# A second wait before the first exponential of every key tile, in a one-core attention kernel

## What is computed

```python
qkv = (x @ Wqkv_w + Wqkv_b).reshape(Bb, Ll, 3, Hh, dd)
scores = einsum('bhid,bhjd->bhij', q, k) * scale
attn = softmax(scores + causal_mask, axis=-1)
y_softmax = einsum('bhij,bhjd->bhid', attn, v)
def step(state, inp):
    q_t, k_t, v_t = inp
    state = retention * state + Gamma * (v_t[..., :, None] * k_t[..., None, :])
    return state, einsum('bhij,bhj->bhi', W_static + state, q_t)
alpha = sigmoid(gelu(x @ gate_w1 + gate_b1) @ gate_w2 + gate_b2)
y = alpha * y_softmax + (1.0 - alpha) * y_stp
x = x + (y @ out_w + out_b)
x = x + fp8_linear(layernorm(x), weight, bias)
```

## Time and profile before

| what | value |
|---|---|
| median of 3 runs | 1900.53 us |
| lowest and highest run | 1897.35, 1902.42 us |
| the profiled execution, its own time | 1900.53 us |
| its span, first to last instruction | 1898.8 us |
| granted TensorE clock, mean | 0.932 |
| PE, DVE, ACT, POOL busy | 89%, 82%, 71%, 64% of the span |
| middle stage, 178.9 to 1735.1 us | 1556.2 us |
| groups 2 and 3 of the middle stage | 379.2 and 382.5 us |

### The profile page before, as it was taken

One profiled execution on the slowest core, in us unless ns is written; L12 is line 12 of the kernel. 1 busy time (PEld: TensorE's weight loads), 2 busy tenths in 40 slices (PEclk: granted clock), 3 DMA queues, 4 the chain that ended last, 5 costly groups with the idle time before them and its releaser, 6 DMA issues. The chain is left out here.

```text
span 1898.8 us, 37291 instructions
## 1 busy us (share of the span) xinstructions
PE 1688.7 (89%) x13680; PEld 603.6 (32%) x13680; DVE 1551.2 (82%) x1709; ACT 1352.6 (71%) x2819; POOL 1223.0 (64%) x1146
## 2 busy tenths in 40 slices
PE   5996699999999999999999999999999999986633
PEld 3542122223333332233333322333323233323522
DVE  4457998998888899988888998989889999802967
ACT  2551288888886888888868887888678888894311
POOL 2102497768777777687777776877777788832535
PEclk9996599999998999999989999999989999997865
DMA  4674342241221421412214213122243121104402
GB/s 137 228 242 136 81 109 80 62 99 55 70 74 56 104 81 61 103 53 69 72 60 103 82 59 96 59 70 64 67 103 91 40 90 49 52 9 137 138 11 77
DMA packets 115176, 162.88 MB, mean 86 GB/s; under 512 B 29808, under 2 KB 57648, under 8 KB 114992
## 3 DMA queue, kind: packets, MB, share of 16 engines
q1 hardware_dynamic: 112608, 158.74, 28.7%
q10 hardware_dynamic: 2384, 1.77, 0.3%
HBM read 122.00 MB, written 38.01 MB: 84 GB/s over the span
## 5 line engine op out<-in xcount | busy, mean ns | idle before, releaser
L1399 DVE TENSOR_REDUCE pmax<-PS 128x2 f32<-128x1024 f32 (+2 forms) x1120 | 1213.6, 1130 | 147.0 <-PE PS L1203 117.1
L1351 ACT ACTIVATE probs<-PS 128x512 f32<-128x512 f32 (+3 forms) x2304 | 1124.6, 572 | 263.6 <-PE PS L1239 188.7
L1239 PE MATMUL PS<-Q_st,K_st 50*128 50x512 f16 (+3 forms) x1408 | 394.2, 366 | 15.8 <-DVE y_sb L1424 4.9
L1203 PE MATMUL PS<-K_st,Q_st 48*128 48x512 f16 (+3 forms) x1408 | 342.5, 362 | 13.4 <-DVE pmax L1399 11.3
L1260 PE MATMUL PS<-probs,V_g 128*17 128x512 f32 (+3 forms) x2816 | 346.1, 564 | 9.1 <-ACT o_t L1372 4.4
L1111 POOL TENSOR_TENSOR v_exp<-v_exp,k_rows 128x512 f32<-128x512 f32 x256 | 321.3, 1284 | 31.1 <-DMA v_exp<-qkv_t 30.4
L1153 POOL TENSOR_TENSOR state<-odd,q_rows 128x514 f32<-128x514 f32 x256 | 281.7, 1132 | 6.1
L1239 PE MATMUL PS<-Q_st,K_first 50*128 50x512 f16 (+3 forms) x896 | 270.5, 381 | 14.4 <-DVE shift L1414 6.9
L1203 PE MATMUL PS<-K_first,Q_st 48*128 48x512 f16 (+1 forms) x832 | 217.9, 406 | 25.3 <-DVE pmax L1399 23.7
L1260 PE MATMUL PS<-probs,V_first 128*17 128x512 f32 (+3 forms) x1792 | 232.4, 591 | 0.0
L1142 POOL COPY carry<-odd 128x4 f32<-128x4 f32 x64 | 12.0, 187 | 329.3 <-DVE odd L1434 329.3
(11 more groups left out here) (167 smaller groups left out, 1500.2 us busy)
## 6 DMA issues: line engine op xcount, KB each, us to landing
v_exp<-qkv_t SPq DMA_DIRECT2D x256, 256.0 KB
qkv_t<-proj SPq DMA_DIRECT2D x24, 512.0 KB, 3.8
qk_parts<-parts SPq DMA_DIRECT2D x16, 512.0 KB, 5.3
Q_st<-qk_parts SPq DMA_DIRECT2D x192, 32.0 KB, 3.8
v_rows<-vaug SPq DMA_DIRECT2D x8, 544.0 KB, 6.1
xin<-x SPq DMA_DIRECT2D x8, 512.0 KB, 6.2
k_rows<-qkv_t SPq DMA_DIRECT2D x16, 256.0 KB, 3.9
q_rows<-qkv_t SPq DMA_DIRECT2D x16, 256.0 KB, 6.2
```

The costliest lines, as they stand in the source:

```text
L1203: mm = pe.matmul(PS[:, bank, 0:width], Q_st[rows, c, pair, j * P:(j + 1) * P], keys[rows, pair, blk * CH:blk * CH + width], start=True, st ...
L1239: mm = pe.matmul(PS[:, bank, 0:CH - r * P], keys[rows, pair, kt * P:(kt + 1) * P], Q_st[rows, c, pair, r * P:CH], start=True, stop=(kt < T ...
L1351: act.activation(probs[:, tile % P_SLOTS, h, 0:CH - r * P], PS[:, step[5], 0:CH - r * P], ACT.Exp, scale=SCORE_SCALE).then_inc(exp_done, 1)
L1399: dve.tensor_reduce(pmax[:, s % 2, pair * TPC + j:GH * TPC:PAIRS * TPC, blk], PS[:, bank:bank + SIDES, 0:width], AX.X, ALU.max).then_inc(m ...
```

## The change

ScalarE gets a wait on `values_done` ahead of head 0's exponential of every key tile, before the wait on `scores_ready` that stands there. It asks for the number that says, with the credit of 3, that V of tile t-3 has ended, the last reader of the slot in `probs` that this exponential writes. Nothing else is edited; all lines from 1351 on stand two lines lower.

```diff
                             if kind == "scores":
                                 tile, h = TILE_AT[s] + step[3], step[4]
                                 r = max(step[3] - TPC * ORDER[s], 0)
+                                if h == 0:
+
+                                    act.wait_ge(values_done, g * TILES + tile + 1)
                                 item = tile * GH + h
-
                                 act.wait_ge(scores_ready, g * GH * TILES + item + 1)
                                 act.activation(probs[:, tile % P_SLOTS, h, 0:CH - r * P], PS[:, step[5], 0:CH - r * P],
                                                ACT.Exp, scale=SCORE_SCALE).then_inc(exp_done, 1)
```

## The result

| | before | changed |
|---|---|---|
| median of 5 runs | 1900.53 us | 1913.37 us |
| lowest and highest | 1895.49, 1902.42 | 1912.23, 1918.02 |
| ratio, 95% interval | | 1.0087 (1.0072 to 1.0103) |
| profiled execution, span | 1898.8 us | 1919.2 us |
| middle stage in the profile | 1556.4 us | 1574.4 us |

What follows compares the result with a forecast made beforehand. The prediction took the closed chain of a plain tile through head 0's exponential, nearly level with VectorE, as the bound. It added 15.4 us for tiles and 0.6 for the table load to 1900.5: 1916.5 us, range 1905 to 1931.

Steps and rivals of the forecast that it cites:

- What bounds the kernel: Middle stage, plain key tile: a closed chain through head 0's exponential takes 2.37 us, each link waiting for the one ahead.
- The condition is never late: Head 0: V of tile t-3 has long ended when the scores come, so as data the wait costs nothing.
- What is added: ScalarE, head 0: `scores_ready` stands alone and the exponential is handed over only afterwards, 0.07 us per late wait.
- Rival C: ScalarE's late lone wait costs VectorE's 0.12 us, or later queuing costs more, and nearly all passes: 1927 to 1939; chance 0.15.
- How many tiles: Middle stage: in 400 of 576 tiles the fourth S loads within 45 ns of the end of head 0's exponential.
- first sum: Middle stage: 400 tiles x 0.07 = 28.0 us if each delay goes through.
- What gives back: Middle stage: TensorE's delay makes VectorE's next lateness smaller, so a share of 0.55 passes, 15.4 us.
- The table load: ScalarE, first exponential: the 1.28 us load moves behind the lone wait and loses its idle cover; 0.6 us, once.
- A (costs nothing): Head 0's wait is satisfied by its data and its hand-over lies beside other work: 1900.5 us; chance 0.07.
- B (VectorE sets the tile): VectorE's lateness at the maxima products ahead of the fourth S hides the delay: 1900.5 to 1906 us; chance 0.07.
- D: Middle stage: changed meeting of engines lessens TensorE's waiting elsewhere and makes the kernel faster, 1894 us; chance 0.03.

Runs made afterwards that it cites:

- the pair with half maxima: Kernel before with VectorE reading half of each product for maxima in the middle stage, without and with the change's wait: 1845.41 and 1878.54 us.
- third wait: Changed kernel plus a long-satisfied wait on `turn_emptied` at head 0, written ahead of `scores_ready`: 1922.11 us, ratio 1.0126 to the kernel before.
- second lone instruction: Kernel before with head 0 waiting on `values_done`, `turn_emptied`, `scores_ready` and `out_turned`, in that order: 1946.02 us, ratio 1.0246 to the kernel before.

## Why the prediction was right, point by point

- **What bounds the kernel.** The chain of 0.42 + 0.60 + 0.05 + 1.30 for a plain tile was right. The changed tile is 2.438 where 2.44 was written, and only the link that was named has grown. With half of VectorE's maxima gone it did not shorten, so VectorE is no part of it.
- **The condition is never late.** Shown by the order of the waits: the same condition, as a lone wait in front, costs nothing (1.0001). The trace of before says it directly: V of tile t-3 had raised `values_done` at least 1.17 us ahead of head 0's scores in every tile.
- **What is added.** The mechanism is shown from both sides: the late wait alone costs, the early one alone does not. The price was taken as 0.07 us, from ends of products that are modelled; measured it is 0.061. The trace of before had that to the nanosecond: counted from the rise of the semaphore, the same two instructions of line 755 start 85 ns after it behind the lone wait and 24 with the wait held, 61 apart. The price of VectorE's row, 0.12, was not it, and that pair is not alike: the lone instruction there (line 1706) raises a semaphore as well. Rival C is out.
- **How many tiles.** 400 x 0.07 = 28.0 was the first sum, called what comes if each delay goes through. With VectorE out of the way the delay cost 31.8 us, that is 31.8 / 0.061 = 521 tiles' worth of 576. So 400 was too low a count as a bound on what may pass, and so was 464: that view counts idle time ahead of all four heads and leaves out tiles in which ScalarE had no recorded idle time and still started when its scores came (four exponentials of 0.60 take 2.06 us, so their records overlap). By the start after the scores it is 525 tiles. The 400 are only those whose fourth S waited for head 0, and part of the rest was held by VectorE: with half the maxima the same count gives 456. That the others pass the delay on through heads 1 to 3, for which the next tile's second and third S wait, is argued; a second or third S waited so in 71 and 105 tiles before.
- **What gives back.** 15.4 us was predicted for the tiles. The 16.5 us measured are 16.5 / 0.061 = 270 tiles' worth, a share of 0.52 of the 521 (the profiled 18.0 gives 0.57), where 0.55 was written. That closeness is in part luck: the counts alone gave 0.43, a little over half was my judgement, and the low count of 400 and the high price of 0.07 in part made up for each other. That VectorE is what gives back is shown by the pair with half maxima; that it falls behind its scan and catches up is what I argued from the trace, and no run took the scan away.
- **The table load.** Its place was predicted and seen; what it is worth, 0.6 us in the sum, is below what the runs can tell.
- **The rivals.** A (costs nothing) fell, but the run with the other order of waits is just the case named in it, and there it holds. B (VectorE sets the tile) fell: 16.5 is above its 5.6, though VectorE took about half. The margin of 0.2 us that B was given was misread: the two products behind the load at 444.55 start at 444.56 and take 0.39 (the row below), so by their modelled ends they are done at 444.95, when the fourth S loads. D needed 22.5 us from somewhere; the 69 tiles that became shorter gave 12.4, and the kernel got slower.

```profile
444.56 0.39 PE L1203 MATMUL PS<-K_st,Q_st 48*128 48x512 f16 x2
```

The time grows with the delay, and how much for each nanosecond hangs on VectorE:

| kernel | head 0 starts after its scores | middle stage | for each ns added |
|---|---|---|---|
| before | 22 ns | 1556.4 us | |
| changed | 83 | 1574.4 | 0.30 us |
| third wait | 104 | 1579.3 | 0.28 |
| second lone instruction | 159 | 1603.2 | 0.34 |
| half maxima: no wait to wait | 22 to 83 | 1500.4 to 1532.2 | 0.52 |

The upper end for one ns would be 0.576 us, one for each tile, or 0.525 for the tiles whose head 0 starts when its scores come. Each row is one profiled execution that may be off by some 5 us, so 0.30, 0.28 and 0.34 can't be told apart with certainty; that the last is higher because VectorE's lateness is used up as TensorE gets slower would fit and is not shown.

## What to carry to other kernels

Where an instruction has two conditions, look at which of them the instruction itself holds: put the one that ends late there, and the one that is long satisfied in front, and the second wait cost nothing here (1.0001). In this kernel the wait that is written first stays on the instruction, so the late one is written first. A lone wait costs in front of an idle engine and hides in front of a busy one, so a wait that "is always satisfied" still has to be placed. To price a small delay, find the closed chain of one iteration in the timeline and ask what runs nearly level beside it: here VectorE gave back 14 of 32 us.

## What the runs showed of the hardware

- A working instruction of ScalarE that held its wait started 22 to 25 ns after the semaphore rose, where the engine was free; behind a lone late wait 82 to 83; with a second condition in the same lone instruction (38 ns long instead of 17) 104; with a second lone instruction 159.
- With a third wait, 1152 added conditions at head 0 became 576 lone instructions: in these kernels a lone instruction held one or two conditions, and the working instruction one. I had expected one each.
- Where the lone wait was satisfied early, ScalarE's exponentials followed each other as before, with 576 lone waits among them, and the kernel took the same time within 0.16%.
- The lone wait in front of the first exponential, which needs another function table, stood in front of the table's load as well: the load of 1.28 us began at 231.63 us instead of 202.94, and the idle time ahead of it no longer hid it.
